# Another order of the scores, the maxima and the copies within the steps of an attention layer

## The reference

```python
# layer 0
y = einsum('nm,bmd->bnd', adj, x)
x = layernorm(x + einsum('bnd,do->bno', y, weight) + bias)
# layer 1: 8 heads of 64 columns, masked where adj == 0
q, k, v = split(x @ w_qkv)
attn = softmax(where(adj == 0, -inf, q @ k.T * 64**-0.5))
o = (attn @ v) @ w_proj + b_proj
x = layernorm(x + o + layernorm(o) * ln_gamma + ln_beta)
```

## Time and profile before

| | before |
|---|---|
| median of three runs | 3760.88 us |
| the profiled execution | 3768.99 us |
| its span, first to last instruction | 3767.2 us |
| mean granted TensorE clock | 0.971 |
| first turn of the second layer | 807.6 us from the start |
| TensorE, VectorE, ScalarE, POOL busy | 3442.6, 2750.1, 2201.0, 1869.5 us |

### The profile page before, as it was taken

The page is one execution under the profiler, slowest core; times in us unless marked ns, Lnnn a source line. Parts: engine busy times, 40 slices in busy tenths (PEclk is TensorE's granted clock), DMA queues, the critical chain, the costliest instruction groups (busy, mean ns, idle before and its releaser), DMA issues.

```text
span 3767.2 us, 87486 instructions
## 1 busy us (share of the span) xinstructions
PE 3442.6 (91%) x31248; PEld 2811.1 (75%) x31248; DVE 2750.1 (73%) x6557; ACT 2201.0 (58%) x4629; POOL 1869.5 (50%) x2559
## 2 busy tenths in 40 slices
PE   8999999989989989999898999999989989999895
PEld 6888888877777777777776777777767777777774
DVE  7666666657777777777777777777767777777776
ACT  4444434446666666666666666666656666666664
POOL 4555555533554544555544454444444454444445
PEclk9999999999999999999999999999999999999997
DMA  6555555530111111111111111111111111111110
GB/s 195 177 176 176 177 178 178 178 115 27 45 47 45 45 46 45 45 47 45 45 45 46 45 45 46 57 45 45 45 45 46 45 52 54 47 47 45 45 36 31
DMA packets 345002, 276.91 MB, mean 74 GB/s; under 512 B 13664, under 2 KB 275808, under 8 KB 344928
## 3 DMA queue, kind: packets, MB, share of 16 engines
q1 hardware_dynamic: 344928, 275.83, 23.9%
HBM read 141.56 MB, written 134.22 MB: 73 GB/s over the span
## 4 chain that ended last, share of the span: by engine, by line
PE 42%; DVE 20%; ACT 19%; issue 13%; POOL 6%; ACTq 0%; DVEq 0%; DMA 0%; SPq 0%; POOLq 0%
PE bank L817 14%; PE bank L311 9%; PE bank L324 8%; DVE pt_lo L1098 7%; ACT pt_hi L990 6%; ACT probs L983 5%; PE bank L824 4%; DVE probs L1082 4%; DVE ot L1118 3%; PE bank L796 3%; DVE o_stats L1126 2%; POOL probs L713 2%; ACT v L999 2%; PE bank L333 1%; DVE o L1143 1%
## 5 line engine op out<-in xcount | busy, mean ns | idle before, releaser
L983 ACT ACTIVATE probs<-probs,bias_row 128x512 f32<-128x512 f32 x1024 | 729.2, 713 | 446.7 <-DVE bias_row L1082 446.7
L1098 DVE TENSOR_TENSOR pt_lo<-bank,pt_hi 128x512 fp32r<-128x512 f32 x1024 | 661.0, 684 | 323.3 <-ACT pt_hi L990 277.8
L990 ACT ACTIVATE pt_hi<-bank 128x512 fp32r<-128x512 f32 x1024 | 548.6, 587 | 281.2 <-PE bank L796 281.2
L713 POOL TENSOR_SCALAR probs<-probs,inv_sums 128x480 f32<-128x480 f32 (+1 forms) x1024 | 700.8, 698 | 0.0
L1082 DVE CUSTOM_DVE_ANT_0 probs<-bank,mask_bias 128x512 f32<-128x512 f32 x1024 | 662.7, 685 | 8.0 <-PE bank L780 4.1
L710 POOL TENSOR_TENSOR probs<-probs,inv_sums 128x32 f32<-128x32 f32 x512 | 122.9, 240 | 1076.7 <-DVE inv_sums L1088 1076.7
L824 PE MATMUL bank<-x_hi,w_hi 64*128 64x512 f32 x1024 | 422.6, 413 | 60.9 <-DVE k_lo L1104 40.6
L824 PE MATMUL bank<-x_hi,w_lo 64*128 64x512 f32 x1024 | 415.2, 405 | 56.9 <-POOL probs L713 56.9
L826 PE MATMUL bank<-x_hi,w_hi 64*128 64x512 f32 x1024 | 422.7, 413 | 0.0
L796 PEld LDWEIGHTS bank<-ident,probs 64*128 64x128 f32 x8192 | 350.7, 142 | 96.3 <-issue 24.1
L817 PE MATMUL bank<-pt_hi,v 64*128 64x512 f32 x2048 | 299.0, 409 | 131.0 <-ACT pt_hi L990 102.8
(11 more groups left out here) (110 smaller groups left out, 10884.3 us busy)
## 6 DMA issues: line engine op xcount, KB each, us to landing
x_in<-in_x_dram SPq DMA_DIRECT2D x32, 1024.0 KB, 5.6
ut_hi<-ut_hi_sb SPq DMA_DIRECT2D x128, 256.0 KB, 3.7
ut_lo<-ut_lo_sb SPq DMA_DIRECT2D x128, 256.0 KB, 3.7
u_beta_rows<-ub SPq DMA_DIRECT2D x32, 1024.0 KB, 4.4
x_hi<-ut_hi SPq DMA_DIRECT2D x128, 256.0 KB, 4.3
x_lo<-ut_lo SPq DMA_DIRECT2D x128, 256.0 KB, 4.6
out_dram<-o SPq DMA_DIRECT2D x128, 256.0 KB, 3.3
ub_row<-u_beta_rows SPq DMA_DIRECT2D x124, 256.0 KB, 2.7
```

The lines of the kernel that those rows point to most:

```text
L713: pool.tensor_scalar(probs[:, k % 2, a, cols], probs[:, k % 2, a, cols], inv_sums[:, k % 4, a:a + 1], 0.0, ALU.mult, ALU.add)\
L983: act.activation(probs[:, k % 2, a, :], probs[:, k % 2, a, :], ACT.Exp, bias=bias_row[:, k % 4, a:a + 1], scale=-1.0, accum_out=sums[:, k ...
L990: act.activation(turned_into(pt_hi, k, i), turned(i), ACT.Copy).then_inc(pthi_made, 1)
L1098: dve.tensor_tensor(turned_into(pt_lo, k, i), turned(i), f32(turned_into(pt_hi, k, i)), ALU.subtract).then_inc(ptlo_made, 1)
```

## The change

- FILL and EARLY are set anew. In parts 1 and 2 no unit stands between the turn and the scores, in part 0 three instead of four. Two more units lie ahead of `attend_v`, and one less each in parts 0 and 2.
- On ScalarE `exponent` moves ahead of `scaled`, of `ot_hi_part` and of the copies of the units, which now stand in parts 1 and 2 behind it (before: in part 1 ahead of it and in part 3 ahead of `pt_hi_part`). `result` moves behind them.
- On VectorE `masked_max` moves ahead of the low parts in parts 1 and 2, with one unit ahead and one behind it in part 2; in parts 0 and 3 it follows the low parts directly and moves ahead of `row_shift` and `ot_sum`. The wait for the scores moves to the reciprocal in part 1 and ahead of the first unit in part 2. Units 2 and 3 stay in part 3.

```diff
--- before.py
+++ after.py
@@ -628,8 +628,8 @@
             S_STEP = [9, 11, 13, 14]
 
 
-            FILL = [(4, 10), (5, 9), (5, 7)]
-            EARLY = (4, 2, 2)
+            FILL = [(3, 10), (0, 14), (0, 12)]
+            EARLY = (3, 4, 2)
             BEFORE = [sum(EARLY) + sum(sum(f) for f in FILL[:n]) for n in range(T - 1)]
             assert sum(EARLY) + sum(sum(f) for f in FILL) == 48
             assert S_STEP[-1] + 1 < STEPS
@@ -1033,23 +1033,20 @@
 
                 def batch(b, last_part=True, more=True):
                     for k in range(STEPS):
-                        if k % T == 3:
-                            unit_hi(b, k, 2, more)
-                            unit_hi(b, k, 3, more)
                         pt_hi_part(b, k)
                         if output_at(b, k, 0) and (last_part or k >= T):
                             ot_halves(*output_at(b, k, 0))
-                        if k % T == 1:
-                            unit_hi(b, k, 0, more)
-                            unit_hi(b, k, 1, more)
-                        if last_part and row_at(k - 1, S_STEP) is not None:
-                            result(b, row_at(k - 1, S_STEP))
+                        if k + 2 < STEPS or more:
+                            exponent(b, k + 2)
                         if last_part and row_at(k, Z_STEP) is not None:
                             scaled(b, row_at(k, Z_STEP))
                         if output_at(b, k, 1) and (last_part or k >= T):
                             ot_hi_part(*output_at(b, k, 1))
-                        if k + 2 < STEPS or more:
-                            exponent(b, k + 2)
+                        if k % T in (1, 2):
+                            unit_hi(b, k, k % T * 2 - 2, more)
+                            unit_hi(b, k, k % T * 2 - 1, more)
+                        if last_part and row_at(k - 1, S_STEP) is not None:
+                            result(b, row_at(k - 1, S_STEP))
 
                 for i in range(2):
                     qk_hi_part(0, i)
@@ -1083,8 +1080,10 @@
                                                  -SCALE, 3.0e38, ALU.add, ALU.min,
                                                  bias_row[:, k % 4, a:a + 1]).then_inc(max_found, 1)
 
-                def inverse(b, k):
+                def inverse(b, k, scores_too=False):
                     dve.wait_ge(exp_made, b * 32 + (2 * k + 2))
+                    if scores_too:
+                        scores_at(b, k + 1)
                     dve.reciprocal(inv_sums[:, k % 4, :], sums[:, k % 4, :]).then_inc(inv_made, 1)
 
                 def scores_at(b, k):
@@ -1109,11 +1108,9 @@
                     dve.tensor_tensor(v[:, n, :, 1, :], g_bank[n][:].rearrange("p (h d) -> p h d", d=HEAD),
                                       f32(v[:, n, :, 0, :]), ALU.subtract).then_inc(vlo_made, 1)
 
-                def ot_sum(b, p, scores_of=None):
+                def ot_sum(b, p):
                     for a in range(2):
                         dve.wait_ge(ot_half, b * 8 + (2 * p + a + 1))
-                        if a == 1 and scores_of:
-                            scores_at(*scores_of)
                         h = slice(a * HEAD, (a + 1) * HEAD)
                         dve.tensor_tensor(ot[h, :], o_bank[a][h, :], ot[h, :], ALU.add).then_inc(ot_summed, 1)
 
@@ -1173,22 +1170,30 @@
                     for k in range(STEPS):
                         group, part = divmod(k, T)
                         ahead = k + 2 < STEPS or more
-                        summed = output_at(b, k, 0) and (last_part or k >= T)
+                        filled = group == 0 or (last_part if group == 1 else more)
+
                         if k + 1 < STEPS or more:
-                            inverse(b, k + 1)
-                        if part >= 2:
-                            unit_lo(b, k, part * 2 - 4, last_part, more)
-                            unit_lo(b, k, part * 2 - 3, last_part, more)
-
-                        pt_lo_part(b, k, ahead and part != 0)
+                            inverse(b, k + 1, ahead and part == 1)
+                        if part == 2:
+                            if ahead and filled:
+                                scores_at(b, k + 2)
+                            unit_lo(b, k, 0, last_part, more)
+                        elif part == 3:
+                            unit_lo(b, k, 2, last_part, more)
+                            unit_lo(b, k, 3, last_part, more)
+                        if ahead and part in (1, 2):
+                            masked_max(b, k + 2, waited=part == 1 or filled)
+                        if part == 2:
+                            unit_lo(b, k, 1, last_part, more)
+                        pt_lo_part(b, k, ahead and part in (0, 3))
+                        if ahead and part in (0, 3):
+                            masked_max(b, k + 2, waited=True)
                         if last_part and row_at(k - 1, S_STEP) is not None:
                             row_shift(b, row_at(k - 1, S_STEP), 1)
                         if last_part and row_at(k, Z_STEP) is not None:
                             row_shift(b, row_at(k, Z_STEP), 0)
-                        if summed:
-                            ot_sum(*output_at(b, k, 0), scores_of=(b, k + 2) if ahead else None)
-                        if ahead:
-                            masked_max(b, k + 2, waited=part != 0 or summed)
+                        if output_at(b, k, 0) and (last_part or k >= T):
+                            ot_sum(*output_at(b, k, 0))
                         if output_at(b, k, 1) and (last_part or k >= T):
                             ot_lo_part(*output_at(b, k, 1))
                         if last_part and row_at(k, O_STEP) is not None:
```

## The result

The changed kernel took 3917.5 us in the median (3907.2 to 3931.1, four runs) against 3767.0 for the kernel before in the same runs (3752.6 to 3778.5): 1.040 times as long, interval 1.035 to 1.046. The forecast was 3801, with a range to 3880: the direction was right, the size was not. The profiled execution took 151 us more than that of before (span 3918.5 against 3767.2), at a mean granted clock of 0.959 (0.971). Medians from here on leave out executions over 1.5% above the fastest of their kernel: one of e1, whose median with it is 3719 (the figure that later expectations use), and four of c1 (3748 with them).

What follows compares the result with a forecast made beforehand. TensorE, busy 91% of the span, was taken to set the pace. Step terms summed to +1.35 us per batch, over 30 batches +40 us; 3769 + 40 - 8 (profiled execution to median) gave 3801 us, range 3735 to 3880.

Steps and rivals of the forecast that it cites:

- Part 2's loss with `pt_lo` last: VectorE's low parts, now last in part 2, hold the next turn: 5.58 us against 4.86, +0.72 per group.
- step 8: `t` ends later behind the exponentials, so POOL's normalise holds turn 9: step 8 at 6.3 us, steps 7-8 +1.1.
- the wait of 3 us for `k_lo`: In step 10 TensorE waits 3 us for VectorE's `k_lo`, which now has two maxima ahead of it.
- Part 3's gain: Unit copies end ahead of the turn, so `pt_hi` runs earlier and `attend_v` needn't wait: 6.22 us instead of 7.62, -1.4.
- steps 9 and 10: VectorE's longer chain behind the reciprocal delays the next turn: +1.35 us per batch, +1.75 with the clock term.
- the clock's +0.4: Step 9 may start at 1.2 GHz after step 8's wait: +0.4 us per batch, bounds 0 and 1.6.
- I take nothing: Waits themselves, eight steps with a new one in a bounded chain: priced at zero instead of 1 us per batch.
- Steps 11 to 13: One POOL chain from `t` to row 3's normalise: 17.9 at full clock, 18.9 at low, taken as 18.6 us, -0.5.
- step 14: Step 14 of each batch: 5.6 to 6.5 us against 6.46 (5.9 in the mean of the batches), -0.2.
- the clock falls more often: Rival: waits in part 2 and steps 12 and 13 bring two more clock falls, +3.2 us per batch: 3895 us; 12%.
- The rows stay hidden: Rival: `t` is early enough for POOL in steps 8 and 10, -3.6 us per batch: 3655 us; 17%.
- cancel: Rival: losses and gains cancel, clock unhurt in step 9 and steps 11-13 at 17.9: +0.25 us per batch, 3770 us; 25%.

Runs made afterwards that it cites:

- e1: Kernel before with only the change's FILL and EARLY (TensorE's order), ScalarE's and VectorE's orders old: 3711 us, 0.986 of the kernel before.
- c1: e5 with VectorE's part 1 also back in the old order, low parts before maxima: 3738 us, 0.990 of the kernel before.
- e3: Changed kernel with VectorE's part 2 in the old order (both units, low parts, then maxima): 3865 us, 1.023 of the kernel before.
- e4: Changed kernel with `scaled` and `ot_hi_part` ahead of the exponentials, shifts ahead of the maxima in parts 0 and 3: 3802 us, 1.008 of the kernel before.
- y: e1 plus VectorE's order of the change, ScalarE's order old: 3942 us, 1.043 of the kernel before.
- w: e1 plus ScalarE's order of the change, VectorE's order old: 4061 us, 1.074 of the kernel before.
- e5: Changed kernel with the edits of e3 and e4 together: 3700 us, 0.980 of the kernel before.
- f2: Changed kernel with two VectorE waits swapped in part 2, the unit's own copy first, then the scores: 3923 us, one execution.
- v1: e1 plus, on VectorE, only part 0's maxima ahead of `ot_sum`: 3632 us, 0.963 of the kernel before.
- x1: v1 with ScalarE's `result` moved to the end of the step, behind the exponentials: 3684 us, 0.974 of the kernel before.
- x2: Changed kernel with ScalarE's `result` moved back ahead of the exponentials, nothing else: 4001 us, 1.059 of the kernel before.

## Why the prediction was right or wrong

*Right.* Part 2's loss with `pt_lo` last (5.74 against 5.58), step 8 (6.26 against 6.3) and the wait of 3 us for `k_lo`. e3 takes away the first (4.66) and shortens step 10, e4 takes away the second (4.47), so these causes are shown.

*Right in size, for another reason.* Part 3's gain (6.27 against 6.22). The prediction put it down to ScalarE's copies of units 2 and 3 now standing behind the exponentials of part 2. They stood there before as well; y has the same 6.27 with ScalarE's old order, and w none of it (8.08) with the new one. The gain is that of VectorE's early maxima.

*Luck in steps 9 and 10.* The forecast of +1.75 against +1.9 is made of two misses. The chain was 0.4 too short: the two steps take 13.7 where step 9 ran at full clock, against 11.91 + 1.35 = 13.26. And the clock's +0.4 was 0.3 too much: step 9 ran at 0.72 in 10 of 29 batches, but step 10 was then mostly shorter, which left 0.1 in the mean.

*Wrong, three terms.* The miss is 3.5 us per batch, 105 of the 111 us by which the profiled executions differ more than forecast.

1. *Small prices in the bounded chains, "I take nothing" for the waits among them:* about +0.8 per batch. Steps 1 and 5 took 4.64 (forecast 4.45), steps 2 and 6 5.74 and 5.83 (5.58). VectorE in step 1:

```profile
2252.22 0.17 DVE L1087 RECIPROCAL inv_sums<-sums 128x2 f32<-128x2 f32 x1 [0.30 <-PE bank L780]
2252.41 0.69 DVE L1079 CUSTOM_DVE_ANT_0 probs<-bank,mask_bias 128x512 f32<-128x512 f32 x1
```

 The maximum follows 0.19 after the reciprocal, not 0.10. That is not the wait's price: in e5's step 13 it is 0.20 as well in the 9 of 29 batches where the reciprocal had not waited. From the end of `pt_lo` to the turn it is 0.45 (2260.67 to 2261.12), not 0.39, since I had taken POOL's handover for VectorE's. And f2 shows 0.10 to 0.19 for the waits behind the new one. The paragraph that named a wait's price, 0.12 for each of eight steps or some 30 us, then set it to zero by rows of low parts whose waits are met when they are reached. Those rows say nothing of a wait behind one that blocks. The trace of before did: behind a reciprocal that had been released late the op on the first unit followed after 0.12 in step 2 (1906.18 to 1906.30) and 0.20 in step 6, against 0.07 where nothing had blocked. The Trainium skill, "VectorE: DVE Perf Modes", section "The DRAIN you can't avoid", speaks of semaphores that ops give one after another; f2 measures another case, and there the measurement decides.

2. *Steps 11 to 13, "I take 18.6", and step 14:* +1.2 and +0.5. The sum followed one POOL chain from the first `t`. The chain that counts runs through turn 12: step 11, then row 3's `t`, which the change puts behind exponentials, then row 3's POOL work. So the terms for full and low clock (17.9 and 18.9) were both too small: the steps took 18.4 in the two batches with step 11 at full clock, 20.0 in those at 0.78. And in 27 of 29 batches part of step 11 ran at the lower of the clock's two levels, 1.2 instead of 2.4 GHz (16 before the change), behind waits of 2.0 to 3.1 us in step 10; the two at full clock followed waits of 1.7 and 1.9. Over the batches the sum follows the low clock of step 11 almost exactly. e4 shows the share of the order: row 3's `t` ends 4.0 after turn 12 instead of 5.7, and at the same clock of 0.78 the three steps take 18.2, not 20.0. What the clock itself costs no run parts from the rest. In step 14 the clock was low as often as before (20 and 19 of 29 batches). There the forecast took about 5.7, which is the step at full clock with the low parts last (5.71 in the other nine batches), and left out that the clock falls in most batches; the mean was 6.23. The low clock doesn't follow from the length of the wait alone: behind the same 1.8 us in step 8, step 9 was low in 10 of 29 batches, and behind the longest waits in step 13 (3.2 us) step 14 was at full clock. The rival "the clock falls more often" (3895) gave this 12% and was the nearest of the four, in part by luck: it had no loop edge, and behind the waits of part 2, which it named, steps 3 and 7 ran at full clock in all batches.

3. *The loop edge was in no term:* +1.0. An edge with a load costs 3.2 us of standstill (38.3 us before the first transposes at 12 edges; 18.3 at before's 4) and 1.6 more in step 0 where the clock is low, behind 9 of the 12. Twelve are some 54 us, before's four some 25. Step 15 without them was right: 6.66 in the median against 6.75. This had been in sight: the timeline of before has a step 15 of 12.0 us, and the group of the transposes shows "issue" ahead of its first. First before, then after (busy, mean ns, idle before):

```profile
L796 PE MATMUL bank<-ident,probs 64*128 64x64 f32 x8192 | 351.0, 226 | 37.0 <-issue 18.3 <-POOL probs L713 15.1 <-DVE pt_lo L1098 3.5
```

```profile
L796 PE MATMUL bank<-ident,probs 64*128 64x64 f32 x8192 | 362.9, 229 | 67.8 <-issue 38.3 <-POOL probs L713 17.5 <-DVE pt_lo L1097 12.0
```

The three give 0.8 + 1.7 + 1.0 = 3.5.

The rival that the page "SBUF — State Buffer" of the Trainium skill suggested by its section "Who interferes with whom" is seen, but small: `ot_lo` beside POOL takes 1.37 (2300.48) as before, and the POOL strip at 2325.83 takes 0.69 instead of 0.24 while `ot_lo` (2325.46) runs. "The rows stay hidden" and "cancel" are out: e4 at 3802 shows what the rows' late work costs.

*Still open:* what decides whether an edge has a load. The counts (2 in e1 and v1, 4 before, 6 or 7 in x1, x2 and y, 12 to 21 in the nine executions where ScalarE has both the copies and `result` behind the exponentials) look like more than chance. Neither move alone brings them (x1 has 7, x2 6), and from x1 to c1 the copies' move takes 7 to 21; no run shows the mechanism.

## What to carry to other kernels

An order within a step is priced over all engines at once. ScalarE's order cost 9% by itself and next to nothing on top of VectorE's; so build the corners of the square (each engine's part alone) before judging the whole, and keep the part that gains. For a chain through the slower engines follow every link that the change moves, not the first alone: each row's `t` was moved, and row 3's was not counted. And where a size comes out right, look whether its cause does: part 3's gain came from another engine's order than was forecast.

## What the runs showed of the hardware

- The branch that closes TensorE's loop (864 matmuls per batch) takes 0.2 us, or 4.4 to 6.5 us when the pass loads its instructions anew (9 packets of 16 KB, 0.15 MB); with twice the body nearly every edge does (3.7 us, 14 of 15, with 15 packets in a pass). The Trainium skill, "Runtime: NRT & Kernel Launch", section "Instruction fetch mechanics", says that a taken branch to a target outside the sequencer's window has to wait for a load. The long edges agree; that most edges of the same loop load nothing it doesn't tell.
- On VectorE one met wait behind a blocking one cost 0.10 us, two cost 0.19, and none in front of it (f2).
- After 9 of the 12 edges with a load the next step ran at a low clock, mostly 0.71 and 5.83 instead of 4.23 us.
- The same wait of TensorE, 1.8 us in step 8 of each batch, was followed by a clock of 0.72 in 10 of 29 batches and by full clock in the others.
